# Idle matmuls in the norms of two interleaved streams: four behind each stream's, or eight behind the second's only

## The reference, cut to what matters

```python
def _layernorm(x, axis=-1, eps=1e-05):
    m = jnp.mean(x, axis=axis, keepdims=True)
    v = jnp.var(x, axis=axis, keepdims=True)
    return (x - m) / jnp.sqrt(v + eps)
...
x = x + jnp.tanh(g_xattn[0]) * _L0_xattn_ref(_layernorm(x, axis=-1), ctx_1024, ctx_1024, ...)
x = x + jnp.tanh(g_ffn[0]) * _L0_ffn_ref(_layernorm(x, axis=-1), ...)
x = x + jnp.tanh(g_xattn[1]) * _L1_xattn_ref(_layernorm(x, axis=-1), ctx_1024, ...)
...
```

## Time and profile before

| | us |
|---|---|
| median of the runs | 1390.13 |
| lowest and highest of three | 1376.54, 1393.41 |
| the profiled execution's own time | 1378.8 |
| its span, from the first to the last instruction | 1377.0 |
| mean granted TensorE clock (1 is full) | 0.861 |

### The profile page before, as it was taken

One profiled execution on the slowest core, in us unless ns is written; L12 is line 12 of the kernel. 1 busy time (PEld: TensorE's weight loads), 2 busy tenths in 40 slices (PEclk: granted clock), 3 DMA queues, 4 the chain that ended last, 5 costly groups with the idle time before them and its releaser, 6 DMA issues. The chain is left out here.

```text
span 1377.0 us, 23880 instructions
## 1 busy us (share of the span) xinstructions
PE 1157.4 (84%) x9146; PEld 828.6 (60%) x9146; DVE 607.4 (44%) x1412; ACT 498.0 (36%) x1182; POOL 367.6 (27%) x328
## 2 busy tenths in 40 slices
PE   5988978888679699789897879898796899888784
PEld 4666755656457576775565666465575656756553
DVE  3544555355433236562554773454231344434322
ACT  2433523344234353341242442143342433234242
POOL 2022041330411404411312231404215170431422
PEclk9997978899889899689697999898798966779797
DMA  9000000000412110000000000400122310000122
GB/s 342 10 1 1 2 4 13 5 15 14 145 53 59 52 36 14 14 1 1 1 2 7 7 8 6 159 2 27 55 58 56 119 34 2 2 30 1 37 75 65
DMA packets 54029, 52.87 MB, mean 38 GB/s; under 512 B 6816, under 2 KB 49312, under 8 KB 53024
## 3 DMA queue, kind: packets, MB, share of 16 engines
q1 hardware_dynamic: 48800, 40.85, 9.2%
q0 software_dynamic: 5120, 10.50, 2.6%
HBM read 34.02 MB, written 17.30 MB: 37 GB/s over the span
## 5 line engine op out<-in xcount | busy, mean ns | idle before, releaser
L374 POOL TENSOR_TENSOR small<-small,neghalf 128x4 f32<-128x4 f32 x56 | 56.9, 1025 | 526.5 <-DVE small L396 315.9
L1583 PEld LDWEIGHTS bank<-wmoe,otx 128*128 128x128 f32 x764 | 108.3, 201 | 100.9 <-issue 90.5
L661 DVE TENSOR_REDUCE mx<-bank 128x8 f32<-128x512 f32 x128 | 88.0, 688 | 150.7 <-PE bank L493 134.8
L1583 PE MATMUL bank<-wmoe,otx 128*128 x764 | 112.9, 288 | 47.3 <-DVE otx L1690 15.5
L1275 POOL DMA_INDIRECT yg<-ybuf,posi x80 | 76.6, 958 | 266.7 <-DMA ybuf<-otx 239.9
L578 ACT ACTIVATE probsT<-bank 128x512 f32<-128x512 f32 x128 | 73.1, 597 | 165.6 <-PE bank L505 159.5
L516 PEld LDWEIGHTS bank<-vblk,probsT 128*64 128x64 f32 x2048 | 80.7, 156 | 40.9 <-ACT probsT L578 22.0
L516 PE MATMUL bank<-vblk,probsT 128*64 128x18 f32 x2048 | 92.6, 227 | 12.9 <-ACT probsT L578 11.0
L505 PE MATMUL bank<-csb,probs 128*128 128x128 f32 x512 | 92.4, 321 | 8.9 <-ACT probs L582 8.2
L299 PE MATMUL bank<-warm_x,warm_w 128*128 128x224 bf16 x540 | 98.4, 287 | 0.0
L1249 POOL DMA_INDIRECT xbuf<-rows,posi x80 | 80.3, 1004 | 66.0 <-DVE ebi L1236 34.7
(11 more groups left out here) (279 smaller groups left out, 2075.5 us busy)
## 6 DMA issues: line engine op xcount, KB each, us to landing
ybuf<-otx SPq DMA_DIRECT2D x122, 64.0 KB
xblk<-xbuf SPq DMA_DIRECT2D x26, 256.0 KB
wmoe<-in_w_moe SPq DMA_DIRECT2D x3, 2048.0 KB
wmoe<-in_w_moe SPq DMA_DIRECT2D x1, 3072.0 KB
xbuf<-otx SPq DMA_DIRECT2D x2, 1472.0 KB, 19.9
wmoe<-in_w_moe SPq DMA_DIRECT2D x1, 1536.0 KB
xbuf<-rows,posi POOLq DMA_INDIRECT x80
yg<-ybuf,posi POOLq DMA_INDIRECT x80
```

The costliest lines, as they stand in the source:

```text
L661: link(c, dve.tensor_reduce(s.mx[:, k % 2, :], s3, AX.X, ALU.max))
L1583: mm = pe.matmul(YB[:, 0:P], aT[:, na % 3, ch * P:(ch + 1) * P], wmoe[:, bass.ds(e * (H * P) + at, P)], start=(ch == 0), stop=(ch == H - 1))
```

## The change

The calls of `keep_warm` in `norm_pe` are given a count of 8 for stream 1 and of 0 for stream 0, in place of 4 for each.

```diff
--- before.py
+++ after.py
@@ -316,7 +316,7 @@
                     pe.matmul(s.pieces[h], C("center"), part[:, h % 2 * T:(h % 2 + 1) * T], start=True, stop=True)\
                       .then_inc(*c.give("centred"))
             if second is None:
-                keep_warm(s, WARM_CENTRE)
+                keep_warm(s, 2 * WARM_CENTRE if s is streams[1] else 0)
             yield
             stat = s.SA if second is not None else s.OY if kind == "both" else s.TP
             if second is not None:
@@ -328,7 +328,7 @@
                                start=True, stop=True, skip_group_check=True)
             mm.then_inc(*c.give("meansq"))
             if kind != "both":
-                keep_warm(s, WARM_MEAN)
+                keep_warm(s, 2 * WARM_MEAN if s is streams[1] else 0)
             yield
             for bank, at in ((s.TP, 0), (s.OY, PC))[:2 if kind == "both" else 1]:
                 pe.wait_ge(*c.next("rooted"))
```

## The result

The change makes the kernel a little slower: 1396.26 us median (20 runs, 1385.67 to 1417.96) against 1385.29 us for the kernel before (20 runs, 1368.96 to 1410.74), ratio 1.0122, 95% interval 1.0087 to 1.0157. Every run also records its mean granted clock, and it was 0.8470 on average after. For the kernel before it is on record for the 139 runs made beside the experiments: 0.8564 on average, with a mean time of 1383.0 us. The difference is 0.0094, with a standard error of 0.0016.

What follows compares the result with a forecast made beforehand. TensorE, 84% busy, was taken to bound the kernel through its queue, waits and clock. Gains of 0.35 and 2.29 less 1.9 lost gave -0.74 us (1378.8 to 1378.1); with run spread the forecast was 1387, range 1369 to 1405.

Steps and rivals of the forecast that it cites:

- the first rival: Stream 0's nine bare norms, stream 1 three steps behind, drop the clock: half +14 us (1401), all +28 (1415); chance 0.20.
- the weighing of the clock: Stream 0's waits without idle matmuls: nearby stretches showed both clock levels, so a wait alone was judged not to decide.
- The queue, -0.74 us: Shifted blocks in TensorE's queue: 0.35 us gained side by side, 2.29 gained and 1.9 lost three steps apart.
- The side-by-side norm: Norms with streams side by side: second spread at most 0.07 us earlier, in five of nine, 0.35 us gained.
- ±5.7: Ends of the queue term if 60 blocks' matmuls counted in one stream only, at full clock: -5.7 to +5.7 us.
- The signs: Trace checks: eight taking 0.76 us, line 336's POOL waits 27 to 31 us, scores 0.8 us after block, clock 0.85 to 0.87.
- Stream 0's second norm: Stream 0's second layer norm, three steps apart: means and spread move up 0.38 us, a gain.
- the third norm: Stream 0's third layer norm, three steps apart: gains nothing, as stream 1's eight end where its centring is released.
- stream 1's eight behind the means: Stream 1's norms, three steps apart: four more lie in waits (1.12, 2.08 us), costing nothing if the wait exceeds 0.38.
- The second rival: Stream 1's long norm waits: eight in a row keep the clock, 2.08 us wait falls to 1.7; -12 us, 1375; chance 0.18.
- The third: Stream 1's eights delay stream 0's scores and softmax, without the 2.29 us gains: +1.9 us, 1389; shares the forecast's 0.62.
- B: Theory from the experiments: stream 1's eights delay what stands behind them in TensorE's queue, whatever the clock; no size given.

Runs made afterwards that it cites:

- a1: The changed kernel run again with no further edit, against the kernel before: 1407.9 us against 1378.59, ratio 1.0184.
- e2: The change made only in pairs 2 and 3, where stream 1 is three steps behind, against the kernel before: 1390.35 us, ratio 1.0045.
- e3: Stream 0's blocks taken away, stream 1's left at four, against the kernel before (120 idle matmuls fewer): 1390.81 us, ratio 1.0092.
- e6: No idle matmuls in the norms of either stream (240 fewer), against the kernel before: 1393.56 us against 1388.37, ratio 1.0032.
- e1: The change made only in pairs 0 and 1, where the streams are side by side, against the kernel before: 1381.39 us against 1378.62, ratio 0.9985.
- e4: Stream 0 kept at four, stream 1 raised to eight, against the kernel before (120 idle matmuls more): 1394.16 us, ratio 1.0116.
- e5: The change mirrored, eight for stream 0 and none for stream 1, against the kernel before: 1395.87 us against 1388.37, ratio 1.0053.
- e7: Eight behind centring and means for both streams (240 more), against the kernel before: 1403.31 us against 1378.59, ratio 1.0203.
- b1: The kernel before, unchanged, run again for a second profile: 1383.79 us against 1387.53, ratio 0.9984.
- e9: The change made only behind the means, four kept behind the centrings, against the kernel before: 1394.0 us, ratio 1.0091.
- e8: The change made only behind the centrings, four kept behind the means, against the kernel before: 1393.76 us, ratio 1.0017.
- e11: The change made only behind the means and only in pairs 2 and 3, against the kernel before: 1389.58 us against 1378.59, ratio 1.0076.
- e14: Stream 0's block behind the means removed in phase 0's second part (16 fewer), against the kernel before: 1401.03 us against 1387.53, ratio 1.0110.
- e10: No idle matmuls behind any centring, four behind all means (144 fewer), against the kernel before: 1380.57 us against 1378.59, ratio 0.9973.
- e16: Stream 0's block behind the means removed in phase 0's second part, run again, against the kernel before: 1378.13 us against 1379.23, ratio 1.0004.

## Why the prediction was wrong

The forecast of no difference is wrong, although 1396.26 us lies in its range: the interval of the ratio excludes 1, and the time came out by the first rival's way, between the forecast and that rival's 1401.

**The step that failed** is the weighing of the clock: "So a wait by itself does not decide", from which the bare norms of stream 0 got 0.20. It rested on two stretches of before at 1.00, 248 to 254 and 288 to 298. Both were stretches in which the blocks still stood. They showed that a wait beside idle matmuls can pass at full clock, and said nothing of one without them. For these two stretches the reading even held. The same work after, the first without an idle matmul in it:

```profile
245.20:250.60 5.40, 4.11 (x38) 3.02 (x36) 1.70 (x4) 2.51 (x6) 1.04 (x1) 1.00 0.01 2
283.83:293.40 9.57, 7.54 (x83) 5.90 (x82) 5.23 (x7) 3.58 (x8) 4.55 (x4) 1.00 0.03 9
```

The first is at 1.00 in all five profiles with both blocks gone. What falls lies at places of which no row was read for this: the "both" norm, which ends just ahead of the second stretch, the routing norm of phase 1, and long stretches that begin elsewhere. One norm of stream 0 (248 to 254) and one of stream 1 (288 to 298) were taken for the nine. A row that warned was there too, 197 to 202 at 0.66 behind a wait of 1.12 us, although a block stood ahead of that wait. What the runs showed in its place: the mean clock of all runs fell by 0.0094, in a1 by 0.0192, in every kernel that bares both of stream 0's blocks in the second parts (e2, e3, e6) by 0.0110 to 0.0148, and in those that leave them there (e1, e4, e5, e7) by at most 0.0016, inside their errors.

**The rival's size.** It had +14 us for half of the nine norms and +28 for all. The drop of the clock is worth 11.0 us over the 20 runs and 22.5 in a1. Its mechanism was told as one fall at each norm's place, 3.1 us each. In the traces the falls at the norms, where there are any, are 0.6 to 1.1 us ("both" norm) and 1.1 to 2.8 us (routing norm), and the rest lies in half-clock stretches that begin elsewhere, 17 us long in after's phase 0 and 48 us in a1's. That the time came out near this rival's half size is luck in part: not half of nine like falls, but a few small ones and a few long stretches.

**The queue, -0.74 us.** At full clock the matched matmuls say -0.8, and a1's +0.4, against a scatter of 4.6 between the two profiles of before. Most single steps came out as read. The side-by-side norm of the earlier trace rows took 6.13 us from the first centring to the second spread (80.47), and takes 6.01 after (71.74 to 77.75), with POOL's two powers still one block (2.02 us for 2.12) and 0.32 us of wait ahead of the second spread:

```profile
71.74 1.99 PE L316 MATMUL bank<-xs,csb 128*128 128x256 f32 x8
73.58 0.93 PE L299 MATMUL bank<-warm_x,warm_w 128*128 128x224 bf16 x8
74.34 1.86 PE L327 MATMUL bank<-csb,probs 128*128 128x1 f32 x16
76.06 0.93 PE L299 MATMUL bank<-warm_x,warm_w 128*128 128x224 bf16 x8
76.82 0.60 PE L336 MATMUL bank<-csb,small 128*128 128x128 f32 x4
77.75 0.65 PE L336 MATMUL bank<-csb,small 128*128 128x128 f32 x4 [0.32 <-POOL small L374]
```

Eight take 0.76 us, as the sign had it, with none between the streams' centrings. Stream 0's second norm lost its 0.38 us, one block of the two taken away:

```profile
246.40 1.13 PE L316 MATMUL bank<-xs,csb 128*128 128x256 f32 x4 [0.41 <-DVE xs L675]
...
248.04 1.05 PE L327 MATMUL bank<-csb,probs 128*128 128x1 f32 x8
249.03 0.65 PE L542 MATMUL bank<-csb,upd 128*128 128x128 f32 x4
250.56 0.65 PE L336 MATMUL bank<-csb,small 128*128 128x128 f32 x4 [0.88 <-POOL small L374]
```

From centring to spread it is 4.16 us where it was 4.54, with the wait at 0.88 for the 0.63 of the earlier trace rows; at the third norm 6.58 us for 6.59, the nothing that was forecast, with 0.80 for the 0.41 of the earlier trace rows. And stream 1's eight behind the means lie in its wait, which is shorter by one block, 0.74 us for the 1.12 of the earlier trace rows:

```profile
192.14 0.93 PE L299 MATMUL bank<-warm_x,warm_w 128*128 128x224 bf16 x8
193.81 0.65 PE L336 MATMUL bank<-csb,small 128*128 128x128 f32 x4 [0.74 <-POOL small L374]
```

Still, over its 20 runs +5.3 ± 1.4 us are left at equal clock, inside the bounds of ±5.7 but not -0.74. With the slope at 13.9 us for 0.01, which the same runs give within a job if the clock is fitted to the time, it would be +3.2. Against its own 20 runs of before it would be +2.2, if their clock was that of the 139. In the matched matmuls +3.6 us lie where both kernels ran at half clock, but 4.0 of that in the experts of phase 1, in which no block was moved. a1's +1.5 ± 2.2 and the sum of e1 and e2, +2.2 ± 3.1, would go with the forecast as well. What of the 5.3 us is the queue's is open.

**The signs.** The waits of line 336 on POOL were to total 27 to 31 us and were 23.8, so more of them was filled than I counted; by how much each of the 27 changed was not traced. They were 26.8 in b1 and 25.3 in a1. Behind stream 1's first centring the scores of line 487 start 1.09 us after the block, not 0.8, as the block began at half clock (187.51 to 188.60). The mean clock was to be 0.85 to 0.87: 0.854 in the profile, yet 0.847 over all runs. The sign that I gave for being wrong, a difference of over 0.02 in the clock of a profile, was far too coarse: half of that is 11.7 us. So was the profile itself: b1's, of the kernel before, has 0.855.

**The second rival**, that stream 1's eights keep the clock, fell: e4 has them without e3's loss, and its clock is before's. Its own place shows the same. The wait of 2.08 us fell to 1.32, further than the 1.7 it had, and behind it the clock was at half for 10.2 us in both kernels (before 351.3 to 361.5, after 355.4 to 365.6):

```profile
354.42 0.65 PE L336 MATMUL bank<-csb,small 128*128 128x128 f32 x4 [1.32 <-POOL small L374]
```

Only e3 against the change leaves room for it (0.0148 against 0.0094, and a1's 0.0192 speaks against). **The third**, that the cover isn't there, had +1.9 us (+1.55, if the 0.35 gained side by side is kept), and at equal clock the change's +5.3 is on its side of zero; B may be a part of the loss.

**The transposes.** The Trainium skill (TensorE: Matmul & The Clock Gate, Part 4: PE-mode transpose) says that transposes don't count as TensorE being busy in the same way. By that rule all nine norms of stream 0 were to fall, which is the first rival at its full size, 28 us; the fall of the clock was worth 11.0. The sign agrees, the size doesn't, and the norm between stream 1's transposes (245.20 to 250.60 after) ran at 1.00 without its cover. That transposes are a reason where the clock did fall isn't shown either: no kernel here had another kind of matmul in their place.

**Short waits.** The Trainium skill (the same page, Part 1, A second HAM failure mode: psum-queue depth-cycling) tells of a kernel in which TensorE idles only briefly, but often enough between groups of matmuls for the clock to swing between its levels. The rows of the routing norm after agree: the waits that they show are 0.75 us at most, and it comes out at half clock. e9 does not, with a wait of 0.80 us there at full clock.

**Open:** what starts the long half-clock stretches of phase 0's second part (before's 328 to 338 in part or whole is at half clock in after, a1, e2, e8, e11 and e14, but not in e3, e6 and e10, which bare stream 0 as well); whether centring or means counts more; and why a fall of the clock comes in one profile of a program and not in the next (the "both" norm in after and a1). The price of the clock in a single kernel also has the chance of its chip and load in it, as e14 and e16 show.

## What to carry to other kernels

An idle matmul has two prices, one in the queue and one in the clock, and a time alone shows only their sum: read the mean granted clock of every run, take off what it is worth (here 11.7 us for 0.01), and the rest is, to a few us, the queue. Where the blocks stand matters more to the clock than how many there are: here stream 0's earned their place, and the same count moved to the stream three steps behind kept nothing. One or two stretches at full clock in which the cover still stands are no evidence that the cover can go everywhere. And a second profile of the unchanged kernel belongs beside every pair of profiles: here its span differs from the first one's by 10.0 us, and that of the changed kernel by 12.4.

## What was unexpected

Adding costs more than removing gives: 120 more idle matmuls cost 16.3 us at equal clock (0.136 each), 120 fewer gave 4.4 us (0.037 each). That the waits take up what is removed would explain it, but e4 added to stream 1 and e3 took from stream 0, and by e7 less e4 the 120 added to stream 0 cost 22.3 - 16.3 = 6.0 us, so it may be the stream as well. The mean clock of the unchanged kernel ran from 0.841 to 0.868 over the 139 runs, by the price above some 32 us between one execution and another, about twice what the change is worth. And one program, in e14 and e16, was 1.1% slower on one chip and even on another, each time by a 95% interval that excludes the other's value.
